# Attention of the chosen tokens: the products with V in three pieces per four heads, the projection by Wo in four pieces, and stacks and turnings beside other heads

## The chip, the cores and the metric

The kernel is one program on one core of a Trainium2 chip. The metric is the device time of one execution in microseconds (us). It is compared as the median of several runs of each kernel.

## The reference, cut to what matters

The program computes `x + attention(layernorm(x)) + sparse_layer(layernorm(x))` for 8192 rows of 512 numbers. The sparse layer picks the 1023 rows with the largest router weight and gives them a full transformer layer. The change lies in the attention of that layer:

```python
def heads(t):
    return t.reshape(b, kc, H, hd).transpose(0, 2, 1, 3)
q = rope(heads(hn @ wq), pos_sel)          # kc = 1023, H = 16, hd = 32
kk = rope(heads(hn @ wk), pos_sel)
v = heads(hn @ wv)
sc = jnp.einsum('bhqd,bhkd->bhqk', q, kk) / np.sqrt(hd)
sc = sc + m_sel[:, None]
a = jax.nn.softmax(sc, axis=-1)
o = jnp.einsum('bhqk,bhkd->bhqd', a, v).transpose(0, 2, 1, 3).reshape(b, kc, d) @ wo
x1 = x_sel + o
x2 = x1 + jax.nn.gelu(rmsnorm(x1, ln2) @ w1) @ w2
```

## The kernel before

The program has three phases, one after the other: the linear attention of all rows, the preparation of the chosen rows (their K, Q, V), and the attention and MLP of the chosen rows. The stage that the change touches is the attention, in a trace from about 1404 to 1745 us.

The 1023 chosen rows are 8 tiles of 128 queries, t = 0 to 7. Each tile goes through 16 heads, h = 0 to 15, against all 1023 keys. Each engine has its own instruction list, written out in this order; nothing is rescheduled, an engine that meets an unfulfilled wait stands. One turn of the loop `for h in range(H)` is called step h below. In step h:

- TensorE (PE) computes the scores of head h+2 into one of two PSUM pairs `Sp` (`score`, L2141; it waits until VectorE has read head h's scores out of the same pair), then perhaps some products with V (`values`, L2167), then turns head h-1's weights in two halves into `Tp[0]` (L2149) and `Tp[1]` (L2153), each half after its copy of the head before has been taken, then perhaps something extra.
- VectorE (DVE) adds the mask to the scores of head h, writes them to `Sm` and finds the least of each row ("the reduce", L2088, 1023 wide), then copies the second half of the turned head h-2 out of `Tp[1]` (`take_t`, L2038), then perhaps something extra.
- ScalarE (ACT) takes the exponential of head h in `Sm` (L1986), then copies the first half of the turned head h-1 (L1959), then perhaps something extra.

The products with V of four heads (a group g; 32 matmuls of 128 rows by 32 columns in fp32, k = 0 to 7 blocks of keys) go into the one PSUM tile `Op`. Before, they are issued in two pieces of 16, k = 0 to 3 and k = 4 to 7, in steps 4g+5 and 4g+6.

All the rest of a tile shares one PSUM tile `Wp`: the four attention groups turned back (`back`, L2177), the rows weighted by 1/sum (`attention_rows` on DVE, L2053) and turned `again` (L2183), the projection by Wo (`project`, L2190, four fp32 matmuls of 512 columns), the residual sum and the second norm on DVE (`second_norm`: step 0 the sum, L2060; step 1 the squares and a first guess of the root; steps 2 and 3 three Newton rounds, 9 tiny instructions, L1362 to L1364; step 4 the scaling, L2071), the normed rows turned (`norm_t`, L2198) for the MLP, and the four query stacks of the next tile (`stack`, L2211; their input `qst` is written by ACT, L1967, and DVE, L2044). The `PTs` buffer holds turned weights of five heads. In the last tile DVE also prepares the finished rows (`keep`, L2075 and L2076).

## Time and profile before

| what | value |
|---|---|
| time, median of 3 runs | 1948.97 us (1943.88 to 1950.05) |
| profiled execution: its time | 1945.36 us |
| profiled execution: its span | 1943.6 us |
| TensorE busy in the span | 95% |
| DVE / ACT busy in the span | 74% / 45% |
| granted TensorE clock, mean | 0.985 |
| attention stage | about 1404 to 1745 us |

The profiled execution is 3.6 us under the median of the runs. Busy shares are means over stages with different limits. In the attention stage every engine follows the same head loop, so its time is read from the starts of instructions: the distance from one start to the next on an engine is what an instruction costs there, also where the printed durations of neighbours overlap.

### The profile page before, as it was taken

What the parts mean: (1) busy time and instruction counts of PE and PEld (TensorE: products, weight loads), DVE (VectorE), ACT (ScalarE), POOL (GpSimd) and SP (SyncE); (2) the same over time, 40 slices, a digit from 0 to 9 for tenths busy, and PEclk for the clock granted to TensorE, in tenths of its full rate; (3) what the DMA queues carried; (4) which work ended last, traced back from release to release, by engine and by line L of the source; (5) the groups of instructions that cost most, each with busy time, mean ns of one, the idle gap of its engine ahead of it and who ended that gap; (6) DMA issues with size and microseconds to landing.
All of it is one profiled execution on the core that took longest, in us unless ns stands there. A gap on an engine that the chain in (4) does not pass through costs nothing. (4 is left out here: it accounts for less than half of the span.)

```text
span 1943.6 us, 72290 instructions
## 1 busy us (share of the span) xinstructions
PE 1848.5 (95%) x32348; PEld 1567.1 (81%) x32348; DVE 1445.2 (74%) x3477; ACT 875.7 (45%) x1494; POOL 148.7 (8%) x179
## 2 busy tenths in 40 slices
PE   6999999999999999999999999879899999879998
PEld 5888888888888888888888888657677777667997
DVE  6888788888887777787777777667588788876222
ACT  4443334343434443444434343325588787764110
POOL 2000000000000000000000000041100000001000
PEclk9999999999999999999999999879999999999999
DMA  4111211121121112111111110236500000015000
GB/s 147 47 46 58 73 52 46 58 74 52 46 74 52 36 36 61 43 36 40 59 41 36 47 51 30 95 95 183 164 26 12 13 12 23 13 41 161 17 12 22
DMA packets 65139, 108.45 MB, mean 56 GB/s; under 512 B 4720, under 2 KB 25216, under 8 KB 64832
## 3 DMA queue, kind: packets, MB, share of 16 engines
q1 hardware_dynamic: 59056, 84.69, 14.0%
q0 software_dynamic: 5776, 19.15, 3.2%
q8 instruction: 256, 4.19, 0.9%
q14 instruction: 51, 0.42, 0.1%
HBM read 59.26 MB, written 27.26 MB: 45 GB/s over the span
## 5 line engine op out<-in xcount | busy, mean ns | idle before, releaser
L1083 PE MATMUL proj<-xnT_high,held 128*128 128x256 f32 x1536 | 235.2, 288 | 3.3 <-DVE xnT_low L782 2.4
L1083 PEld LDWEIGHTS proj<-xnT_high,held 128*128 128x128 f32 x1536 | 203.6, 191 | 9.2 <-DVE xnT_low L782 2.9
L444 POOL TENSOR_TENSOR xs<-xs 128x512 f32<-128x512 f32 x63 | 80.9, 1285 | 1170.0 <-DVE xs L885 1170.0
L1083 PE MATMUL proj<-xnT_low,held 128*128 128x256 f32 x1024 | 163.7, 281 | 0.0
L2088 DVE CUSTOM_DVE_ANT_0 Sm<-Sp,held 128x1023 f32<-128x1023 f32 x128 | 155.5, 1216 | 8.0 <-DVE xs L2076 2.0
L1986 ACT ACTIVATE Sm<-Sm,least 128x1023 f32<-128x1023 f32 x128 | 146.7, 1146 | 14.1 <-DVE least L2088 13.3
L1083 PEld LDWEIGHTS proj<-xnT_low,held 128*128 128x128 f32 x1024 | 140.1, 190 | 0.0
L2141 PE MATMUL Sp<-KS,held 128*128 128x512 f32 x256 | 94.4, 451 | 29.9 <-DVE least L2088 25.6
L506 ACT ACTIVATE Pq<-Pq 128x1024 f32<-128x1024 f32 x63 | 66.9, 1062 | 123.4 <-DVE Pq L848 123.3
L486 ACT ACTIVATE QT<-proj 128x512 f32<-128x512 f32 x64 | 38.1, 595 | 182.4 <-PE proj L1083 182.4
L2038 DVE COPY PTs<-Tp 128x512 f32<-128x512 f32 x128 | 88.3, 690 | 29.7 <-PE Tp L2153 29.2
L465 ACT ACTIVATE DV<-proj 128x512 f32<-128x512 f32 x64 | 38.2, 598 | 160.1 <-PE proj L1093 160.1
L2362 PEld LDWEIGHTS Sp<-held,KS 128*128 128x128 f32 x768 | 95.3, 190 | 6.1 <-issue 3.6
L1959 ACT ACTIVATE PTs<-Tp 128x512 f32<-128x512 f32 x128 | 76.2, 595 | 52.4 <-PE Tp L2149 49.2
L2362 PE MATMUL Sp<-held,KS 128*128 128x256 f32 x768 | 96.8, 282 | 2.6 <-PEq L1863 2.0
L2422 PE MATMUL yb<-w2m,held 128*128 128x512 f32 x384 | 94.5, 396 | 0.0
L486 ACT ACTIVATE KT<-proj 128x512 f32<-128x512 f32 x64 | 38.2, 598 | 99.8 <-PE proj L1083 99.8
L2422 PEld LDWEIGHTS yb<-w2m,held 128*128 128x128 f32 x384 | 70.2, 189 | 14.9
L2149 PE MATMUL Tp<-ident,Sm 128*128 128x128 f32 x512 | 81.0, 281 | 1.0 <-ACT PTs L1959 0.9
L1083 PE MATMUL proj<-xnT_high,wk_low 128*128 128x256 f32 x512 | 81.2, 280 | 0.0
L2153 PE MATMUL Tp<-ident,Sm 128*128 128x128 f32 x512 | 77.4, 274 | 1.6 <-DVE PTs L2038 1.6
L848 DVE TENSOR_TENSOR Pq<-S,mx 128x1024 f32<-128x1024 f32 x63 | 77.2, 1225 | 2.1
(343 smaller groups left out, 4341.2 us busy)
## 6 DMA issues: line engine op xcount, KB each, us to landing
VS<-DV SPq DMA_DIRECT2D x64, 264.0 KB, 3.9
xs<-in_x SPq DMA_DIRECT2D x32, 512.0 KB, 4.8
out_rows<-xs SPq DMA_DIRECT2D x64, 256.0 KB, 2.0
mask_columns<-x1T SPq DMA_DIRECT2D x16, 512.0 KB, 5.2
xs<-in_w SPq DMA_DIRECT2D x16, 512.0 KB, 3.8
xe<-in_x SPq DMA_DIRECT2D x15, 512.0 KB, 3.5
QT<-in_wqT SPq DMA_DIRECT2D x1, 1024.0 KB, 6.5
KT<-in_wkT SPq DMA_DIRECT2D x1, 1024.0 KB, 9.4
```

Source lines behind the costliest of these rows:

```text
L444: pool.tensor_tensor(Ass[k], T1s[k], T2s[k], ALU.add).then_inc(s_as, 1)
L486: act.activation(raw[:, pn, 2 * k:2 * k + 2, :], v, ACT.Copy, scale=scale)
L848: dve.tensor_tensor(Pqs[k].rearrange("p g j k -> p j g k"), s_half(a), mx[:, :, :].rearrange("p j (g o) -> p j g o", o=1).broadcast_to([P, ...
L1083: ins = pe.matmul(bank[:, g * BT:g * BT + BT], w[hw][:, c, o:o + P], xnT[hx][:, c, :], start=n + c == 0, stop=n == 2 and c == G - 1)
L1986: act.activation(Sm[:, h % 4, 0:KC], Sm[:, h % 4, 0:KC], ACT.Exp, bias=least[:, h % 4:h % 4 + 1], scale=-1.0, accum_out=rsum[:, b, h:h + 1 ...
L2038: dve.tensor_copy(PTs[:, slot(t, h), 4:8, :], Tp[1][:, :].rearrange("p (k q) -> p k q", k=4))\
L2088: dve.tensor_tensor_reduce(Sm[:, h % 4, 0:KC], Sp[h % 2][:, 0:KC], mc[:, b, 0:KC], 1.0, 3.0e38, ALU.add, ALU.min, least[:, h % 4:h % 4 + 1])\
L2141: ins = pe.matmul(Sp[h % 2][:, u * 512:u * 512 + 512], QS[:, h, :], KS[:, h, u * 512:u * 512 + 512], start=True, stop=True)
L2149: ins = pe.transpose(Tp[0][:, k * P:k * P + P], Sm[:, h % 4, k * P:k * P + P], ident[:, :])
L2153: ins = pe.transpose(Tp[1][:, (k - 4) * P:(k - 4) * P + P], Sm[:, h % 4, k * P:k * P + P], ident[:, :])
L2362: ins = pe.matmul(self.hb[n % 4][:, e * self.NT:e * self.NT + self.NT], self.w1[hw][:, c, f * P:f * P + P], self.xT[hx][:, c, :], start=m ...
L2422: ins = pe.matmul(yb[(u % 2) * QU + q][:, :], gT[hg][:, n % 4, e, q * P:q * P + P], w2[hw][:, f, :], start=f + m == 0, stop=f == FC - 1 an ...
```

## The change

What it does, for a tile t (steps are those of tile t unless another is named):

- The products with V of a group go in three pieces, of 12, 12 and 8 matmuls, in steps 4g+5, 4g+6 and 4g+7. The first piece waits for ACT's copies alone, the second for DVE's too. ACT's `take_o` follows one step later. `PTs` is split into two tensors, one for each writer, with 5 and 6 slots.
- The projection goes in four pieces of one matmul, in steps 9 to 12, in place of one piece in step 8. `back` moves from step 3 to 6 and `again` from 6 to 7.
- The stacks of the next tile, all in steps 10 to 13 before, go to step 4 (first), 14 and 15 (second and third) and to step 0 of the next tile (fourth). ACT writes `qst` in step 1 in place of step 0; DVE's part stays in step 2.
- `norm_t` moves from step 15 to step 2 of the next tile but one loop turn (`norm_t(t - 2)` in tile t).
- On DVE, `attention_rows` moves from step 5 to step 7 and ahead of that step's copy; `second_norm` steps 0, 1, 2 move from steps 9, 10, 13 to 13, 14, 15, and its steps 3 and 4 from steps 13 and 14 to step 0 of the tile after.

```diff
-SLOTS = 5
-PTs = sb("PTs", [P, SLOTS, Q, P], c=c2_)
+QH = Q // 2
+SLOTS = (5, 6)
+PIECES = ((0, 1, 2), (3, 4, 5), (6, 7))
+PARTS = len(PIECES)
+PTs = [sb(f"PTs{e}", [P, SLOTS[e], QH, P], c=c2_) for e in range(2)]
...
-            if h == 2 and before:
+            if h == 3 and before:
                 take_o(t - 1, G - 1)
-            if h in (6, 10, 14):
+            if h in (7, 11, 15):
                 take_o(t, h // 4 - 1)
             if h > 0:
                 take_t(t, h - 1)
             elif before:
                 take_t(t - 1, H - 1)
-            if h == 1 and before and t >= 2:
+            if h == 0 and before:
+                take_stack(t, G - 1)
+            if h == 1 and after:
+                stack(t + 1)
+            if h == 2 and before and t >= 2:
                 take_x1(t - 2)
-            if h == 7 and before:
+            if h == 4 and after:
+                take_stack(t + 1, 0)
+            if h == 8 and before:
                 take_on(t - 1)
-            if h == 0 and after:
-                stack(t + 1)
-            if 10 <= h < 14 and after:
-                take_stack(t + 1, h - 10)
+            if h == 14 and after:
+                take_stack(t + 1, 1)
+            if h == 15 and after:
+                take_stack(t + 1, 2)
...
+            if h == 7 and before:
+                attention_rows(t - 1)
             if h > 1:
                 take_t(t, h - 2)
             elif before:
                 take_t(t - 1, H - 2 + h)
                 if h == 1:
                     weights(t - 1, 1 - b)
+            if h == 0 and t >= 2:
+                second_norm(t - 2, 3)
+                second_norm(t - 2, 4)
             if h == 2 and after:
                 stack(t + 1)
-            if h == 5 and before:
-                attention_rows(t - 1)
-            if h == 9 and before:
+            if h == 13 and before:
                 second_norm(t - 1, 0)
-            if h == 10 and before:
+            if h == 14 and before:
                 second_norm(t - 1, 1)
-            if h == 13 and before:
+            if h == 15 and before:
                 second_norm(t - 1, 2)
-                second_norm(t - 1, 3)
-            if h == 14 and before:
-                second_norm(t - 1, 4)
-            if not after and (h < Q - 2 or h == 13):
+                if not after:
+                    second_norm(t - 1, 3)
+                    second_norm(t - 1, 4)
+            if not after and (h < Q - 2 or h == 14):
                 keep(min(h, Q - 2))
...
         if part == 0:
+            pe.wait_ge(s_oc, t * G + (g + 1))
             pe.wait_ge(s_ta, t * H + (4 * g + 5))
+        if part == 1:
             pe.wait_ge(s_td, t * H + (4 * g + 5))
-            pe.wait_ge(s_oc, t * G + (g + 1))
-        for k in range(part * (Q // 2), (part + 1) * (Q // 2)):
+        for k in PIECES[part]:
+            e = k // QH
             n = P if k < Q - 1 else P - 1
             for j in range(4):
                 h = 4 * g + j
                 ins = pe.matmul(Op[DK * j:DK * j + DK, 0:P], V[0:n, k, h * DK:h * DK + DK],
-                                PTs[0:n, slot(t, h), k, :], start=k == 0, stop=k == Q - 1)
-        if part == 1:
-            ins.then_inc(s_pv, 1)
+                                PTs[e][0:n, slot(t, h, e), k % QH, :], start=k == 0, stop=k == Q - 1)
+        ins.then_inc(s_pv, 1)
 
     def back(t):
         pe.wait_ge(s_oc, t * G + (G + 1))
-        if t:
+        if t < Q - 2:
+            pe.wait_ge(s_qs, (t + 2) * G + 1)
+        else:
             pe.wait_ge(s_x1, t)
...
-    def project(t):
-        pe.wait_ge(s_w, 16)
-        pe.wait_ge(s_otc, t + 1)
-        for g in range(G):
+    def project(t, gs):
+        if gs[0] == 0:
+            pe.wait_ge(s_w, 16)
+            pe.wait_ge(s_otc, t + 1)
+        for g in gs:
             ins = pe.matmul(Wp[:, :], OnT[:, g, :], wo[:, g, :], start=g == 0, stop=g == G - 1)
-        ins.then_inc(s_wo, 1)
+        if gs[-1] == G - 1:
+            ins.then_inc(s_wo, 1)
...
-    def stack(t, g, first=False):
-
+    def stack(t, g):
 
         if g == 0:
             pe.wait_ge(s_ql, t + 1)
-            if not first:
-                pe.wait_ge(s_xc, t - 1)
+        if g == 0 and t > 2:
+            pe.wait_ge(s_x1, t - 2)
+        elif g == 1 and t > 1:
+            pe.wait_ge(s_xc, t - 1)
         else:
             pe.wait_ge(s_qs, t * G + g)
         for j in range(4):
...
-            if h % 4 in (1, 2) and h > 2:
-                values(t, (h - 5) // 4, h % 4 - 1)
-            elif h in (1, 2) and before:
+            if h % 4 and h > 3:
+                values(t, h // 4 - 1, h % 4 - 1)
+            elif h % 4 and before:
                 values(t - 1, G - 1, h - 1)
             if h > 0:
                 turn_p(t, h - 1)
             elif before:
                 turn_p(t - 1, H - 1)
-            if before and h == 3:
+            if h == 0 and before:
+                stack(t, G - 1)
+            if h == 2 and t >= 2:
+                norm_t(t - 2, True)
+            if h == 4 and after:
+                stack(t + 1, 0)
+            if h == 6 and before:
                 back(t - 1)
-            if before and h == 6:
+            if h == 7 and before:
                 again(t - 1)
-            if before and h == 8:
-                project(t - 1)
-            if after and 10 <= h < 14:
-                stack(t + 1, h - 10, first=not before)
-            if before and h == 15:
-                norm_t(t - 1, after)
+            if 9 <= h < 13 and before:
+                project(t - 1, (h - 9,))
+            if h >= 14 and after:
+                stack(t + 1, h - 13)
...
     turn_p(Q - 1, H - 1)
-    values(Q - 1, G - 1, 0)
-    values(Q - 1, G - 1, 1)
+    norm_t(Q - 2)
+    for part in range(PARTS):
+        values(Q - 1, G - 1, part)
```

On PE the order around the projection shows the first two points. Before, from step 7 on in a middle tile (`Sp` scores, `Op` products with V, `Tp` turned heads, `Wp<-wo` projection):

```order
L2141 MATMUL Sp<-KS,held 128x512 x2
L2149 MATMUL Tp<-ident,Sm 128x128 x4
L2153 MATMUL Tp<-ident,Sm 128x128 x4
L2141 MATMUL Sp<-KS,held 128x512 x2
L2149 MATMUL Tp<-ident,Sm 128x128 x4
L2153 MATMUL Tp<-ident,Sm 128x128 x4
L2190 MATMUL Wp<-wo,OnT 128x512 x4
L2141 MATMUL Sp<-KS,held 128x512 x2
L2167 MATMUL Op<-PTs,V 32x128 x16
L2149 MATMUL Tp<-ident,Sm 128x128 x4
L2153 MATMUL Tp<-ident,Sm 128x128 x4
```

The changed kernel on PE, the last rows of step 9 to step 12 of the same tile:

```order
L2206 MATMUL Wp<-wo,OnT 128x512
L2153 MATMUL Sp<-KS,held 128x512 x2
L2181 MATMUL Op<-PTs,V 32x128 x12
L2161 MATMUL Tp<-ident,Sm 128x128 x4
L2165 MATMUL Tp<-ident,Sm 128x128 x4
L2206 MATMUL Wp<-wo,OnT 128x512
L2153 MATMUL Sp<-KS,held 128x512 x2
L2181 MATMUL Op<-PTs,V 32x128 x8
L2161 MATMUL Tp<-ident,Sm 128x128 x4
L2165 MATMUL Tp<-ident,Sm 128x128 x4
L2206 MATMUL Wp<-wo,OnT 128x512
L2153 MATMUL Sp<-KS,held 128x512 x2
```

The projection no longer stands as one block; one matmul of it follows the turned head of each of four steps, and three of these steps also hold a piece of the products with V.

On DVE the order around the end of a tile shows the norm. Before, the end of step 13 and step 14 (`ISA Sm` is the reduce, `COPY PTs` the copy, `t<-r`, `t<-t,v`, `r<-t,r` one Newton round; the last of three rounds is shown, and the scaling of step 14 behind it):

```order
L1362 SCALAR_TENSOR_TENSOR t<-r 128x1
L1363 TENSOR_TENSOR t<-t,v 128x1
L1364 SCALAR_TENSOR_TENSOR r<-t,r 128x1
L2088 ISA Sm,least<-Sp,held 128x1023
L2088 ISA least 128x1
L2038 COPY PTs<-Tp 128x512
L2071 SCALAR_TENSOR_TENSOR On<-xs,r,ln 128x512
L2088 ISA Sm,least<-Sp,held 128x1023
```

The changed kernel on DVE, the last Newton round of step 15, step 0 of the next tile and step 1 up to the reduce of step 2:

```order
L1364 SCALAR_TENSOR_TENSOR r<-t,r 128x1
L2097 ISA Sm,least<-Sp,held 128x1023
L2097 ISA least 128x1
L2047 COPY PTs<-Tp 128x512
L1362 SCALAR_TENSOR_TENSOR t<-r 128x1
L1363 TENSOR_TENSOR t<-t,v 128x1
L1364 SCALAR_TENSOR_TENSOR r<-t,r 128x1
L2080 SCALAR_TENSOR_TENSOR On<-xs,r,ln 128x512
L2097 ISA Sm,least<-Sp,held 128x1023
L2097 ISA least 128x1
L2047 COPY PTs<-Tp 128x512
L2058 RECIPROCAL rinv<-rsum 128x16
```

The third Newton round and the scaling now stand in step 0, directly ahead of the steps that hold the reciprocal and DVE's part of the next query stack.

On ACT the write of `qst` (`held<-xs`) moves behind one more exponential and copy. In the changed kernel, steps 1 and 2:

```order
L1989 ACTIVATE Sm,rsum<-Sm,least 128x1023
L1962 ACTIVATE PTs<-Tp 128x512
L1970 ACTIVATE held<-xs 128x16x64
L1989 ACTIVATE Sm,rsum<-Sm,least 128x1023
L1962 ACTIVATE PTs<-Tp 128x512
L1983 ACTIVATE x1T<-Wp 128x4x128
```

Before, the same write stood behind the copy of step 0. It now stands one step ahead of the DVE instruction that reads its result.

## Rows read from the trace of the kernel before

**Rows 1.** The page, its first line: the span.

```profile
span 1943.6 us, 72290 instructions
```

**Rows 2.** Windows, one tile: busy us (instructions) by engine, then PEclk, DMA share, GB/s.

```profile
1549.53:1590.93 41.40, 39.17 (x454) 29.89 (x453) 34.53 (x66) 32.63 (x59) 0.95 (x1) 1.00 0.05 14
```

**Rows 3.** Waits of 1400 to 1745 us: total us, times, longest.

```profile
DVE PTs L2038 <- PE Tp L2153: 29.2, 42, 1.2
PE Sp L2141 <- DVE least L2088: 25.6, 53, 1.8
...
DVE xs L2060 <- PE Wp L2190: 19.2, 7, 2.7
```

**Rows 4.** Timeline of PE: start, us, line, operands [idle before, releaser]; steps 1 to 6.

```profile
1571.89 0.60 PE L2153 MATMUL Tp<-ident,Sm 128*128 128x128 f32 x4
...
1575.64 0.70 PE L2141 MATMUL Sp<-KS,held 128*128 128x512 f32 x2 [0.65 <-DVE least L2088]
1576.18 0.60 PE L2149 MATMUL Tp<-ident,Sm 128*128 128x128 f32 x4
1576.62 0.60 PE L2153 MATMUL Tp<-ident,Sm 128*128 128x128 f32 x4
1577.06 0.60 PE L2177 MATMUL Wp<-ident,OTs 128*128 128x128 f32 x4
1577.41 0.71 PE L2141 MATMUL Sp<-KS,held 128*128 128x512 f32 x2
...
1579.23 0.71 PE L2141 MATMUL Sp<-KS,held 128*128 128x512 f32 x2 [0.23 <-DVE least L2088]
1579.87 1.08 PE L2167 MATMUL Op<-PTs,V 128*32 128x128 f32 x32
1580.88 0.66 PE L2149 MATMUL Tp<-ident,Sm 128*128 128x128 f32 x4
...
1581.73 0.71 PE L2141 MATMUL Sp<-KS,held 128*128 128x512 f32 x2
```

**Rows 5.** Timeline of DVE, steps 2 and 3 of the same tile.

```profile
1572.53 0.69 DVE L2038 COPY PTs<-Tp 128x512 f32<-128x512 f32 x1 [0.64 <-PE Tp L2153]
1573.13 1.22 DVE L2044 TENSOR_TENSOR held<-xs,held 128x1024 fp32r<-128x1024 f32 x1
1574.27 1.22 DVE L2088 CUSTOM_DVE_ANT_0 Sm<-Sp,held 128x1023 f32<-128x1023 f32 x1
...
1575.41 0.69 DVE L2038 COPY PTs<-Tp 128x512 f32<-128x512 f32 x1
```

**Rows 6.** Timeline of PE, the projection (step 8) in two tiles.

```profile
1546.50 3.60 PE L2190 MATMUL Wp<-wo,OnT 128*128 128x512 f32 x8
1549.53 1.02 PE L2141 MATMUL Sp<-KS,held 128*128 128x512 f32 x2
...
1587.90 3.60 PE L2190 MATMUL Wp<-wo,OnT 128*128 128x512 f32 x8
```

**Rows 7.** Timeline of DVE, the norm in steps 9 to 14.

```profile
1550.13 0.69 DVE L2060 TENSOR_TENSOR xs<-Wp,xs 128x512 f32<-128x512 f32 x1 [2.74 <-PE Wp L2190]
...
1553.23 0.68 DVE L2063 CUSTOM_DVE_ANT_0 On<-xs 128x512 f32<-128x512 f32 x1
...
1554.52 1.22 DVE L2088 CUSTOM_DVE_ANT_0 Sm<-Sp,held 128x1023 f32<-128x1023 f32 x1 [0.21 <-DVE r L1360]
...
1559.91 0.15 DVE L1362 SCALAR_TENSOR_TENSOR t<-r 128x1 f32<-128x1 f32 x1
...
1561.83 1.22 DVE L2088 CUSTOM_DVE_ANT_0 Sm<-Sp,held 128x1023 f32<-128x1023 f32 x1 [0.21 <-DVE r L1364]
...
1563.58 0.74 DVE L2071 SCALAR_TENSOR_TENSOR On<-xs,r,ln 128x512 f32<-128x512 f32 x1
```

**Rows 8.** Timeline of ACT, steps 0 and 1: copy and `qst`.

```profile
1569.15 0.60 ACT L1959 ACTIVATE PTs<-Tp 128x512 f32<-128x512 f32 x1
1569.65 1.05 ACT L1967 ACTIVATE held<-xs 128x1024 fp32r<-128x1024 f32 x1
```

**Rows 9.** Timeline of DVE, end of tile 7: last reduce, last copy.

```profile
1738.34 1.22 DVE L2088 CUSTOM_DVE_ANT_0 Sm<-Sp,held 128x1023 f32<-128x1023 f32 x1
...
1742.57 0.69 DVE L2038 COPY PTs<-Tp 128x512 f32<-128x512 f32 x1 [0.96 <-PE Tp L2153]
```

More of the change, by code:

```diff
@@ L1909, in feed_forward, with slot, read_before @@
             KC = K - 1
-            def slot(t, h):
-                return (t * H + h) % SLOTS
-            def read_before(eng, t, h):
-                n = t * H + h - SLOTS
+            def slot(t, h, e):
+                return (t * H + h) % SLOTS[e]
+            def read_before(eng, t, h, e):
+                n = t * H + h - SLOTS[e]
                 if n >= 0:
-                    eng.wait_ge(s_pv, n // 4 + 1)
+                    eng.wait_ge(s_pv, n // 4 * PARTS + 2 + e)
             def tile(t):
@@ L1957, in take_t @@
                     act.wait_ge(s_t, t * (2 * H) + (2 * h + 1))
-                    read_before(act, t, h)
-                    act.activation(PTs[:, slot(t, h), 0:4, :], Tp[0][:, :].rearrange("p (k q) -> p k q", k=4),
+                    read_before(act, t, h, 0)
+                    act.activation(PTs[0][:, slot(t, h, 0), :, :], Tp[0][:, :].rearrange("p (k q) -> p k q", k=4),
                                    ACT.Copy).then_inc(s_ta, 1)
                 def take_o(t, g):
-                    act.wait_ge(s_pv, t * G + (g + 1))
+                    act.wait_ge(s_pv, PARTS * (t * G + g + 1))
                     act.activation(OTs[:, g, :], Op[:, 0:P], ACT.Copy).then_inc(s_oc, 1)
@@ L2036, in take_t @@
                     dve.wait_ge(s_t, t * (2 * H) + (2 * h + 2))
-                    read_before(dve, t, h)
-                    dve.tensor_copy(PTs[:, slot(t, h), 4:8, :], Tp[1][:, :].rearrange("p (k q) -> p k q", k=4))\
+                    read_before(dve, t, h, 1)
+                    dve.tensor_copy(PTs[1][:, slot(t, h, 1), :, :], Tp[1][:, :].rearrange("p (k q) -> p k q", k=4))\
                        .then_inc(s_td, 1)
@@ L2254, in _ @@
                 again(Q - 1)
-                project(Q - 1)
+                project(Q - 1, range(G))
                 up.hidden(pe, 2)
```

## The prediction

> **What bounds the kernel now.** First the page for the size of things: a span of 1943.6 us [rows 1], of which the stage that is changed has about 340 (the table above). Then the windows: one tile lasts 41.40 us, which is also the distance between two projections, 1546.50 to 1587.90 [rows 6], at full granted clock (1.00, the 2.4 GHz level), with PE busy 39.17, DVE 34.53, ACT 32.63 us [rows 2]. PE looks full, but then the waits: 53 times its scores waited for the reduce on DVE, 25.6 us in all, while DVE waited 42 times for turned heads (29.2 us) and seven times 2.7 us for the projection [rows 3]. So the stage is a pair of engines that take turns, and a busy share says too little. The timeline gives the rules of the turns.
>
> PE, start to start: a score takes 0.55 (1575.64 to 1576.18), the first half of a turned head 0.44, the second 0.36 when a score follows, so a light step is 1.35. Something of four transposes behind it adds 0.44 (1576.62 to 1577.06 to 1577.41). A step with 16 products with V takes 2.50 (1579.23 to 1581.73), 1.15 more: 1.01 for the products (1579.87 to 1580.88) and 0.14 for the joint. [rows 4] The projection takes 3.03 plus 0.31, since the score behind it lasts 1.02 in place of 0.71, so 3.34 [rows 6].
>
> DVE: the reduce of step h starts at R. The score of step h on PE starts at R + 1.37 or later (1574.27 to 1575.64) [rows 4, 5]. The copy starts at R + 1.15 or 0.64 after the second half of the turned head of PE's step before starts (1571.89 to 1572.53), whichever is later, and costs 0.60 [rows 4, 5]. So DVE needs 1.78 per step without extras, more than PE's light step of 1.35; and DVE can't run ahead, since `Sp` has two buffers.
>
> A tile of before walked by these rules, step 9 to step 9 of the next tile, comes out as the trace has it: starts of the scores within 0.05 us, and 41.4 in all. PE's own work in that is 16 x 1.35 + 8 x 1.15 + 7 x 0.44 + 3.4 = 37.3; the other 4.1 are stalls in steps 2, 4, 7, 10, 13, 15 and 0. This is the tool for the forecast.
>
> **The change, part by part.** All for one middle tile.
>
> Products with V: 12, 12 and 8 matmuls cost 0.76, 0.76 and 0.51 by the 1.01 for 16, and a joint of 0.14 each: steps of 2.25, 2.25 and 2.00. Four more joints: +0.56 on PE. Projection: four pieces of 0.84 and a boundary of 0.08 each (0.44 in place of 0.36 in front): 0.92 each, +0.3. PE's work becomes 16 x 1.35 + 8 x 0.90 + 4 x 0.65 + 7 x 0.44 + 4 x 0.92 = 38.2. The bound from below for joints is nothing.
>
> A rule of the Trainium skill speaks against these joints (TensorE: Matmul & The Clock Gate, Architectural detail: the array is 16x 32x32): the queue pulls weight loads ahead of matmuls in flight. By it the split would be free and PE's work would stay at 37.3. The row shows 0.14 at each border of differing groups, so I take that.
>
> DVE, extras in order, each start to start: residual sum 0.61, squares and first guess 1.29 (1553.23 to 1554.52), nine Newton instructions 1.92 of which 0.19 is the last wait, so three cost 0.58 and six with the wait 1.34; scaling 0.66, by its 0.74 less the overlap of 0.08 that the copy shows [rows 7]; its part of the query stack 1.14 [rows 5]. Their sum hardly changes. Their places do: the residual sum to step 13, then 1.29 in 14, 1.34 in 15, 0.58 + 0.66 = 1.24 in step 0, the reciprocal (an unmoved cost, 0.46 in the walk) in step 1, 1.14 in step 2. Before, the norm stood in steps 9, 10, 13 and 14, three of which hold products with V.
>
> ACT: `qst` now follows the copy of step 1. In the walk PE's first half of step 1 starts 1.40 after the score, the copy about 0.7 after that, 0.50 later `qst` starts and takes 1.05 [rows 8]; DVE, ready for its part 3.1 after the score of step 1, gets it at 3.65. That is a new wait of 0.5 us per tile, and the reduce of step 3 stands behind it on DVE. Before, `qst` was done a whole step earlier.
>
> **The walk.** Starts of the scores, step 9 at 0. Steps 9 to 12 are PE's: 3.17, 6.34, 9.26, 11.52 for steps 10 to 13. The long waits for the projection on DVE and ACT go, as intended, since it no longer stands in a block. The sum on DVE starts at 11.8, the reduce of step 14 at 12.4, the score at 13.79. From here DVE sets the pace, and its reduces start at 15.94, 19.06, 22.08, 24.32 and, behind the new wait, 28.24 for steps 15, 0, 1, 2, 3. The scores follow at 17.31, 20.43, 23.45, 25.70, 29.61, with stalls on PE of 0.8, 0.7, 1.2 and, in step 2, 1.2. Step 3 and 4: 29.61, 31.61; step 5 at 33.86 after a stall of 0.46 (a light step behind one with products, as now); 36.11; 38.80; in step 7 PE turns its head only after DVE has weighted the rows and then copied (0.4), step 8 at 41.65, again light (0.4), step 9 at 43.43.
>
> So a tile takes 43.4 in place of 41.4: 38.2 of work and 5.3 of stalls against 37.3 and 4.1. **+2.0 us a tile.** Behind the evening out of PE stands an uneven DVE: between the reduces of steps 14 and 3 it needs 15.8 us, PE has 11.9 us of work there; between 3 and 13 it is the other way round.
>
> Ends: tile 0 has no norm and no projection. The walk gives the wait for `qst` (+0.45) and then a gain from the pieces, 0.8 by its end, and step 3 of tile 1 starts 0.5 earlier than before. Five tiles from there to step 3 of tile 6: 5 x 2.03 = +10.1, so +9.6. In tile 7 step 0 holds the scaling and last round beside `keep`: +1.3; `attention_rows` leaves step 5: -0.6; steps 6 to 9 with neither block: -1.9; the remainder of the way to that tile's first reduce +0.5. At step 9: +8.9. At its end the last reduce comes 10.3 later; the norm of tile 6 now stands whole behind it (2.4 us of round and scaling), so the last copy starts 5.6 after that reduce where it was 4.2 (1738.34 to 1742.57) [rows 9]: +1.4. The MLP then starts as before, its first products wait for that chain. Sum: 10.3 + 1.4 = **+11.7 us**. The profiled execution took 1945.36, 3.6 less than the median; against the median of 1948.97 this gives 1960.7.
>
> **Rivals.** (A) As walked: 1960.7; own range 1955 to 1966, by joints free (-1.6 in the stage) or steps of the ACT chain adding half a microsecond a tile more. (B) Joints free and ACT's copy earlier, so no wait for `qst`: 7 x 0.5 + 1.6 less, +6.6, 1955.6; with each of three stalls a little smaller, +4, 1953. For it: the 0.14 is read at one kind of border. Against it: a score, a transpose and a product all show such a border. (C) It evens out: the 2.7 us a tile that DVE waited for the projection, and the stall of PE in the steps behind it, go and come back in the same size elsewhere: 1949. (D) Faster: only PE counts. Then a tile is 38.2 of work and 1.3 of stalls in steps 4, 7 and 8, 39.5, so -1.9 for each of six tiles: 1938. It is decided in steps 14 to 2: DVE would have to be 4 us shorter there, or its reduce be let ahead. For it: 29.2 us of DVE's waits [rows 3] do lie in steps with products. Against it: these waits are spare time of an engine that now gets its extras where none is spare. (E) ACT late as well: its exponentials of steps 0 and 2 slide behind `take_stack` and `qst` until PE waits for them, +1 a tile more: 1968. In the walk they keep 1 us and more of slack.
>
> **The numbers.** Chances: A 0.69, B 0.13, C 0.05, D 0.08, E 0.05. A change of 0.3%, 5.8 us, is about what a measurement of this kernel can tell from none. B falls half under it, so faster 0.08, same 0.12, slower 0.80. The range 1950 to 1968 holds A, B and most of E and leaves out D and half of C.
>
> **What would show it.** Right: a tile of 43 to 43.8 us between two projections; PE waits for the reduce in steps 14 to 2 of 0.5 to 1 us, shown shorter by 0.24 than the stall (0.23 shown for 0.47 here [rows 4]); DVE without idle time there except before its query stack part; no 2.7 us wait before the residual sum. Wrong: a tile under 41.4, so the reduce must be able to start before the extras' time has passed; or DVE idle in steps 15 to 2. If the wait before DVE's part of the stack is absent, the price falls by 3.5 us.

## The result, and the profile after

| kernel | median of runs, us | ratio to before | 95% interval |
|---|---|---|---|
| before | 1949.51 (1943.88 to 1958.05) | | |
| after | 1962.14 (1960.49 to 1966.93) | 1.0062 | 1.0046 to 1.0078 |

The change costs 12.1 us; +11.7 and 1960.7 were predicted. The profiled execution took 1961.97 us, close to its median, at a mean granted clock of 0.983 (before 0.985). First the page of after, its first line and the first line of its busy times (engine, busy us, share, instructions):

```profile
span 1960.2 us, 72291 instructions
PE 1858.5 (95%) x32348; PEld 1564.8 (80%) x32348; DVE 1445.5 (74%) x3477; ACT 878.5 (45%) x1494; POOL 148.8 (8%) x179
```

The shares are those of before; they tell nothing. One tile does. The windows of after: the same tile as in [rows 2], then two parts of it, from step 15 to the start of step 3 and from there to step 9 (length; busy us of PE, PE's weight loads, DVE, ACT, POOL; granted clock, DMA share, GB/s):

```profile
1551.54:1595.10 43.56, 40.19 (x453) 29.29 (x453) 34.63 (x67) 33.16 (x61) 0.94 (x1) 1.00 0.05 14
1569.00:1582.00 13.00, 10.62 (x126) 7.79 (x129) 11.24 (x26) 10.59 (x18) 0.85 (x1) 1.00 0.15 42
1582.00:1595.00 13.00, 12.69 (x150) 9.67 (x142) 10.38 (x19) 10.56 (x21) 0.00 (x0) 1.00 0.01 2
```

The tile takes 43.56 us in place of 41.40 at the full granted clock (1.00, the 2.4 GHz level); DVE's busy time is the same to 0.1 us, PE's is 1.0 more, and PE's idle time is 3.37 where it was 2.23. What came to the idle time lies in the first part: there PE is idle for 2.38 of 13.00 us, in the other for 0.31. The same two parts of the tile of before:

```profile
1565.71:1575.64 9.93, 8.99 (x111) 6.75 (x110) 8.77 (x15) 9.06 (x17) 0.95 (x1) 1.00 0.17 54
1575.64:1590.93 15.29, 14.82 (x140) 11.05 (x141) 11.91 (x20) 12.17 (x22) 0.00 (x0) 1.00 0.01 2
```

The waits of after, 1400 to 1765 us (total, times, longest):

```profile
DVE PTs L2047 <- PE Tp L2165: 50.1, 64, 1.5
...
PE Sp L2153 <- DVE least L2097: 28.9, 41, 2.6
...
DVE On L2062 <- PE Wp L2192: 9.2, 8, 2.5
...
DVE held L2053 <- ACT held L1970: 3.4, 6, 0.6
...
DVE xs L2069 <- PE Wp L2206: 1.2, 7, 0.2
```

Beside [rows 3]: the wait for the projection has gone, as intended (19.2 us, now 1.2). But the wait for turned heads has grown from 29.2 to 50.1, and two new ones stand beside it, for the groups turned back (`On`) and for ACT's part of the query stack (`held`). The four rows of DVE add up to 63.9; 2.5 of this (the longest wait for `On`) lies behind the stage, where before has the same wait outside the window of its rows, so 61.4 compares with the 48.4 of the two rows of before. DVE has the same work in a longer stage, so it waits more, only for something else. PE's own wait has grown from 25.6 to 28.9 in fewer, longer pieces (41 for 53), printed 0.24 shorter each than the stall.

The timeline of PE in after, step 9, and then the scores at the start of steps 15, 0, 1, 2 and 3 of the same turn (start, us, line, operands, count [idle before, releaser]):

```profile
1551.54 0.71 PE L2153 MATMUL Sp<-KS,held 128*128 128x512 f32 x2 [0.16 <-DVE least L2097]
1552.18 0.86 PE L2181 MATMUL Op<-PTs,V 128*32 128x128 f32 x24
1552.98 0.66 PE L2161 MATMUL Tp<-ident,Sm 128*128 128x128 f32 x4
1553.47 0.60 PE L2165 MATMUL Tp<-ident,Sm 128*128 128x128 f32 x4
1553.90 1.02 PE L2206 MATMUL Wp<-wo,OnT 128*128 128x512 f32 x2
1554.37 1.03 PE L2153 MATMUL Sp<-KS,held 128*128 128x512 f32 x2
...
1568.79 0.71 PE L2153 MATMUL Sp<-KS,held 128*128 128x512 f32 x2 [0.58 <-DVE least L2097]
...
1571.87 0.71 PE L2153 MATMUL Sp<-KS,held 128*128 128x512 f32 x2 [0.33 <-DVE least L2097]
...
1574.86 0.70 PE L2153 MATMUL Sp<-KS,held 128*128 128x512 f32 x2 [0.97 <-DVE least L2097]
...
1577.14 0.71 PE L2153 MATMUL Sp<-KS,held 128*128 128x512 f32 x2
...
1581.18 0.70 PE L2153 MATMUL Sp<-KS,held 128*128 128x512 f32 x2 [1.08 <-DVE least L2097]
```

And DVE in steps 0 to 3:

```profile
1570.49 1.22 DVE L2097 CUSTOM_DVE_ANT_0 Sm<-Sp,held 128x1023 f32<-128x1023 f32 x1 [0.21 <-DVE r L1364]
...
1571.64 0.69 DVE L2047 COPY PTs<-Tp 128x512 f32<-128x512 f32 x1
1572.25 0.15 DVE L1362 SCALAR_TENSOR_TENSOR t<-r 128x1 f32<-128x1 f32 x1
...
1572.82 0.76 DVE L2080 SCALAR_TENSOR_TENSOR On<-xs,r,ln 128x512 f32<-128x512 f32 x1
1573.49 1.22 DVE L2097 CUSTOM_DVE_ANT_0 Sm<-Sp,held 128x1023 f32<-128x1023 f32 x1
...
1577.42 0.69 DVE L2047 COPY PTs<-Tp 128x512 f32<-128x512 f32 x1 [0.50 <-PE Tp L2165]
1578.67 1.23 DVE L2053 TENSOR_TENSOR held<-xs,held 128x1024 fp32r<-128x1024 f32 x1 [0.56 <-ACT held L1970]
1579.81 1.21 DVE L2097 CUSTOM_DVE_ANT_0 Sm<-Sp,held 128x1023 f32<-128x1023 f32 x1
```

From 1570.49 to 1573.49 DVE goes without a pause from the reduce of step 0 through its copy, three Newton instructions and the scaling to the reduce of step 1, and the score on PE stands 1.37 behind each reduce (1573.49 to 1574.86). Then, behind a wait of 0.50 for a turned head that wasn't foretold (1577.42), the predicted new wait: 0.56 before DVE's part of the query stack, on ACT's part; the reduce of step 3 comes behind it, and PE's wait of 1.08 behind that.

Starts of the scores, step 9 at 0, as predicted and as they came:

| step | 11 | 13 | 14 | 15 | 0 | 1 | 2 | 3 | 5 | 7 | 9 |
|---|---|---|---|---|---|---|---|---|---|---|---|
| predicted | 6.34 | 11.52 | 13.79 | 17.31 | 20.43 | 23.45 | 25.70 | 29.61 | 33.86 | 38.80 | 43.43 |
| after | 5.97 | 11.10 | 13.70 | 17.25 | 20.33 | 23.32 | 25.60 | 29.64 | 33.96 | 38.96 | 43.56 |
| before | 6.37 | 9.96 | 13.68 | 16.18 | 18.44 | 20.18 | 22.72 | 26.11 | 29.70 | 35.14 | 41.40 |

After and before are level at step 14. The loss of a tile arises from there to step 3 (+3.5, in 15.9 us), and 1.4 of it comes back from step 3 to step 9.

Below, "the stage" is the time from the first score to the first MLP product, read from each kernel's trace, and "a tile" is the distance of step 9 of two middle tiles. The median less the stage is 1607.6 us before (1608.1 with the later median) and 1607.2 after, and 1604.3 to 1609.8 over all kernels here, so the stage explains the medians to within about 3 us. (1948.97 is the first median of before, from 3 runs; 1949.51 the one with the runs that came later.)

Stage and tile are read from one execution of each kernel. The tile is the steadier of the two: the middle tiles of after differ by 0.02 us, and experiment 6 repeats them (43.55). The medians are coarser. Of the experiments built on after, only the ratios of 3, 5 and 9 have intervals apart from that of after (1.0046 to 1.0078); those of 1, 2, 6, 7 and 11 overlap it. What a single edit is worth is therefore shown by the tile, and by the stage with the reserve above, not by the median.

### The profile page after: what moved, and what is told of

The parts are those of the page before. It is cut to its first block and busy times, and to the rows that moved or that the text cites. A ratio compares the mean times of both kernels' runs of the same rounds, so it can differ in the third digit from the quotient of the medians.

```text
span 1960.2 us, 72291 instructions
## 1 busy us (share of the span) xinstructions
PE 1858.5 (95%) x32348; PEld 1564.8 (80%) x32348; DVE 1445.5 (74%) x3477; ACT 878.5 (45%) x1494; POOL 148.8 (8%) x179
## 5 line engine op out<-in xcount | busy, mean ns | idle before, releaser
L2153 PE MATMUL Sp<-KS,held 128*128 128x512 f32 x256 | 101.8, 481 | 33.9 <-DVE least L2097 28.9
L2047 DVE COPY PTs<-Tp 128x512 f32<-128x512 f32 x128 | 88.1, 689 | 50.3 <-PE Tp L2165 50.1
L2153 PEld LDWEIGHTS Sp<-KS,held 128*128 128x128 f32 x256 | 41.8, 194 | 60.4 <-issue 50.6
L486 ACT ACTIVATE KT<-proj 128x512 f32<-128x512 f32 x64 | 38.2, 598 | 100.2 <-PE proj L1083 100.2
```

The lines of the kernel that those rows point to most:

```text
L486: act.activation(raw[:, pn, 2 * k:2 * k + 2, :], v, ACT.Copy, scale=scale)
L2047: dve.tensor_copy(PTs[1][:, slot(t, h, 1), :, :], Tp[1][:, :].rearrange("p (k q) -> p k q", k=4))\
L2153: ins = pe.matmul(Sp[h % 2][:, u * 512:u * 512 + 512], QS[:, h, :], KS[:, h, u * 512:u * 512 + 512], start=True, stop=True)
```

## The experiments

**1. The stack's input a step earlier.** ACT writes its part `qst` in step 0 in place of 1. Nothing else.

```diff
-                        if h == 1 and after:
+                        if h == 0 and after:
                             stack(t + 1)
```

> The changed kernel, with ACT's write of the next tile's query stack back in step 0 (behind the fourth stack's copy). Theory (uneven DVE plus a new wait for this write): the idle time of DVE before its part of the stack (3.4 us in 6 waits in the changed kernel) goes, and with it 0.5 us in each of 7 tiles: -3.5 us, a tile of 43.0 us. Rival (the wait is not on the path, PE's more numerous groups are the price): no change, a tile stays at 43.55.

Measured: 1957.3 us, ratio 1.0042 (1.0025 to 1.0059), stage -3.3 (351.72), a tile 42.90 (-0.65). No wait of DVE on `qst` is left. The wait was real and cost about what the prediction said (0.5 a tile, 3.5 in the stage).

**2. The norm where DVE waits.** The three Newton rounds and the scaling of tile t-2 move to steps 10 and 11 of tile t; its turning `norm_t` and ACT's copy move to step 13. In the last tile the rounds and scaling of tile 5 stand in step 0, those of tile 6 in step 15 as in after. Waits keep `h2` of one tile from being overwritten.

```diff
-                        if h == 0 and t >= 2:
+                        if h == (10 if after else 0) and t >= 2:
+                            second_norm(t - 2, 2)
+                        if h == (11 if after else 0) and t >= 2:
                             second_norm(t - 2, 3)
...
                         if h == 15 and before:
-                            second_norm(t - 1, 2)
                             if not after:
+                                second_norm(t - 1, 2)
```

> The changed kernel, with the Newton rounds and the scaling of a tile's norm moved out of steps 15 and 0 into steps 10 and 11 of the next tile, where DVE stands idle, and the turning of the normed rows from step 2 to step 13 (tile 7 apart). No instruction is added or left out, one wait is. Theory (uneven DVE): the walk gives a tile of 41.5 us in place of 43.5, for five tiles: -9.5 us. Rival (PE's joints are the price): -1 us at most, since PE's list holds the same groups. Rival (the steps 10 and 11 have no room): slower.

Measured: 1958.73 us, ratio 1.0053 (1.0036 to 1.007), stage -6.05 (348.94), a tile 41.98 (-1.57). Right in direction, but 9.5 was expected: the tile gave 1.57 of 2.0, the stage 6.05, and the medians of after and of this kernel differ by 3.4 only (by the ratios 1.8), so that the gain in the program's time isn't shown by itself. Five tiles of 1.57 are 7.9; the interval from tile 6 to 7 gave 1.8 back (51.06 in place of 49.22), where the last tile holds more of the norms of two tiles. And the wait for `qst` doesn't shrink when DVE comes sooner, DVE waits for ACT as before. The timeline of DVE in this kernel, steps 2 and 3:

```profile
1571.93 0.69 DVE L2047 COPY PTs<-Tp 128x512 f32<-128x512 f32 x1 [0.64 <-PE Tp L2168]
1573.18 1.23 DVE L2053 TENSOR_TENSOR held<-xs,held 128x1024 fp32r<-128x1024 f32 x1 [0.56 <-ACT held L1970]
1574.33 1.22 DVE L2098 CUSTOM_DVE_ANT_0 Sm<-Sp,held 128x1023 f32<-128x1023 f32 x1
```

**3. Both edits together.**

> The changed kernel with both edits of the two runs before. Theory: the two prices add, a tile of 41.0 us, -13 us against the changed kernel, about 1949 and so level with the kernel before. Rival (the waits hide behind one another): no more than the larger of the two alone.

Measured: 1951.33 us, ratio 1.0011 (1.0000 to 1.0022), stage -10.45 (344.54), a tile 41.33 (-2.22). A tile is as short as before the change; with the late `qst` gone and the norm where DVE waits, three quarters of the stage's loss of 13.6 are gone. The two gains add up to the hundredth (0.65 + 1.57 = 2.22). This isn't yet what moving the norm had cost, for the place that it has here is better than the one before the change, as the next run shows.

**4. The same idea in the kernel before.** There DVE waited 2.7 us for the projection in each tile. Now it does three parts of the norm of tile t-2 in that time, and nothing of it in steps 13 and 14.

```diff
+                        if h == 9 and 2 <= t < Q - 1:
+                            for step in (2, 3, 4):
+                                second_norm(t - 2, step)
...
-                        if h == 13 and before:
+                        if h == 13 and t >= Q - 2:
                             second_norm(t - 1, 2)
```

> The kernel before, in which only the norm is moved: its Newton rounds and scaling from steps 13 and 14 to step 9 of the next tile, ahead of the residual sum, where DVE waits 2.7 us for the projection as one block; the turning of the normed rows follows in step 9. Theory (what counts is where DVE's extras stand): a tile of 40.6 in place of 41.4 us in five tiles, -4 us against the kernel before. Rival (PE is the bound and DVE's extras are covered): no change. Rival (the longer chain in step 9 delays the residual sum and the stacks): slower by 1 to 3 us.

Measured: 1945.51 us, ratio 0.9988 (0.9975 to 1.0001), stage -1.1 against before (340.32), a tile 40.85 (-0.55); the interval of the ratio holds 1. The tile is near what was expected, the stage isn't. From step 3 of tile 1 to step 3 of tile 6 it gains 2.6 us; 0.3 are lost in the stage's first steps, where the code is that of before, 0.2 between step 3 of tile 6 and step 9 of tile 7, and 0.95 behind that, where the last tiles hold more of the norm. The timeline of DVE shows the idle time filled; before, the same sum had 2.74 in front [rows 7]:

```profile
1546.42 0.75 DVE L2072 SCALAR_TENSOR_TENSOR On<-xs,r,ln 128x512 f32<-128x512 f32 x1
1547.51 0.69 DVE L2060 TENSOR_TENSOR xs<-Wp,xs 128x512 f32<-128x512 f32 x1 [0.34 <-PE Wp L2196]
```

**5 and 6. The same load in two places.** Six tiny dependent instructions on DVE whose result nobody uses, once in step 15, where DVE is said to set the pace, and once in step 10, where it waits. The kernel is after; the two differ by one number.

```diff
+                        if h == 15 and before:
+                            for _ in range(6):
+                                link(dve.tensor_tensor(spare[:, :], spare[:, :], spare[:, :], ALU.mult))
```

> The changed kernel with six tiny DVE instructions added in step 15 of tiles 1 to 7, each waiting for the one before (about 0.19 us each, 1.2 in all, the size of two Newton rounds); their result is used by nothing. Theory (DVE sets the pace from step 14 to 3): +1.2 us in each of 7 tiles, +8 us against the changed kernel, a tile of 44.7. Rival (PE sets it everywhere): no change.

> The same six instructions in step 10 of tiles 1 to 7, where DVE is idle for 1.3 us per tile in the changed kernel. Theory: no change against the changed kernel (within 1 us). Rival (any DVE work counts): +8 us as in step 15.

Measured, step 15: 1971.03 us, ratio 1.0113 (1.0095 to 1.0131), stage +9.4 (364.42), a tile 44.69 (+1.13). Step 10: 1961.55 us, ratio 1.0070 (1.0054 to 1.0086), stage +0.2 (355.19), a tile 43.55 (the same). Where the load of step 10 went, the waits tell: DVE waits 40.6 us for turned heads here, 50.1 in after. The timeline of DVE, step 10:

```profile
1552.65 0.69 DVE L2048 COPY PTs<-Tp 128x512 f32<-128x512 f32 x1 [0.86 <-PE Tp L2170]
1553.26 1.12 DVE L2116 TENSOR_TENSOR spare<-spare 128x1 f32<-128x1 f32 x6
1554.59 1.22 DVE L2098 CUSTOM_DVE_ANT_0 Sm<-Sp,held 128x1023 f32<-128x1023 f32 x1 [0.21 <-DVE spare L2116]
```

This separates the two accounts most sharply. If PE alone counted (rival D), neither would cost anything; if DVE's sum counted, both would. The two kernels ran together, and their medians are 9.5 us apart. (Of the +9.4 in the stage 7.0 have come by step 9 of tile 7, about six tiles of 1.13; the 2.4 behind it are 1.3 more than the one load that is left, which wasn't traced further.)

**7. Products with V in two pieces again, in after** (`back` then in step 5).

```diff
-            PIECES = ((0, 1, 2), (3, 4, 5), (6, 7))
+            PIECES = ((0, 1, 2, 3), (4, 5, 6, 7))
...
-                        if h % 4 and h > 3:
+                        if h % 4 in (1, 2) and h > 3:
```

> The changed kernel with the products with V again in two pieces of 16 (steps 4g+5 and 4g+6), the turning back in step 5; projection, stacks, norm and buffers as in the changed kernel. Theory: the pieces hardly matter, since half of them lie in steps in which DVE sets the pace: -0.4 us a tile, -3 us against the changed kernel. Rival (the four more joints a tile are the price): their 0.56 us a tile and the stalls behind them go, and most of the loss with them. Rival (the pieces are a gain): slower.

Measured: 1959.77 us, ratio 1.0057 (1.0042 to 1.0073), stage -3.5 (351.51), a tile 42.80 (-0.75). The gain lies between step 3 and step 9 (-0.9; the other part loses 0.1), and perhaps not all of it is the pieces'. The run also moves `back` from step 6 to 5, and with this goes a wait that DVE has in step 7 of after, in seven tiles together 6.8 us:

```profile
1590.78 0.69 DVE L2062 TENSOR_TENSOR On<-Wp,rinv 128x512 f32<-128x512 f32 x1 [0.89 <-PE Wp L2192]
```

The copy and the reduce of step 8 stand behind it (1591.99), and the score 1.37 behind that (1593.36), so step 7 takes 2.86 where PE has 2.44 of work (2.00 + 0.44). Walked by the prediction's rules without this wait, step 7 ends 0.4 earlier, and of that 0.3 is left at step 9, where the copy of step 8 waits for its turned head instead. So up to 0.3 of the 0.75 may be the place of `back`, an estimate; no run moves it alone.

**8. Products with V in three pieces, in before** (`PTs` split, `back` in step 4, `take_o` a step later, all else as before).

> The kernel before with the products with V in three pieces alone (two PTs tensors, ACT's copies of the groups one step later, the turning back in step 4). Theory, by the walk: a tile of 42.1 in place of 41.4 us, +5 us against the kernel before: steps of 2.25 and 2.00 where DVE already sets the pace, and the joints on PE. Rival (evening out the products removes DVE's waits): -3 us or more. Rival (neither): no change.

Measured: 1954.46 us, ratio 1.0041 (1.0026 to 1.0057), stage +8.5 against before (349.92), a tile 42.56 (+1.16; two of the middle intervals are 42.8). Expected were 0.7 a tile and 5 us; what came is more than the joints. A step that was light and now holds a third piece takes 2.50 in place of 1.77 (step 11) or 2.06 in place of 1.77 (step 3), and the two others, made 4 products lighter each, don't give that back: by step 5 the tile is 1.2 late (30.89 for 29.70, step 9 at 0).

**9. After, with all three undone or mended**: the stack's input in step 0, the norm in steps 10 and 11 (tiles 6 and 7 keep their own parts), V in two pieces. Of the change this leaves the projection in four pieces, the separate `PTs` buffers and the new places of the stacks, of `again` and of `attention_rows`.

> The changed kernel with the query stack's write in step 0 of ACT, the rounds and the scaling of the norm in steps 10 and 11 of the next tile (tiles 6 and 7 apart, which stay as in the changed kernel) and the products with V in two pieces. Left of the change: the projection in four pieces and the places of the stacks and turnings. Theory: the gains of the single runs add up, a tile of 40.6 us and the stage from the first score to the first MLP product at 339 us, against 355.0 in the changed kernel and 341.4 before: -2 us against the kernel before. Rival (once DVE is relieved PE waits elsewhere): between 341 and 345 us, no gain over before.

Measured: 1945.66 us, ratio 0.9981 (0.9971 to 0.9990), stage 338.32, a tile 40.61. Of its waits, 1400 to 1765 us, the one of PE for the reduce is a third shorter than in after (28.9):

```profile
PE Sp L2157 <- DVE least L2098: 18.8, 38, 2.6
```

**10. Before, as in 4, with DVE's part of the query stack in step 7**, ahead of that step's copy, out of step 2.

```diff
+                        if h == 7 and after:
+                            stack(t + 1)
...
-                        if h == 2 and after:
-                            stack(t + 1)
```

> The kernel before with the norm in the idle step 9, as in the run before of that name, and also DVE's part of the next query stack moved from step 2 to step 7 ahead of its copy, where DVE waits 0.7 us for a turned head. Theory: the stall of 0.9 us behind step 2 goes, 0.5 comes back behind step 7: a tile of 40.5 in place of 40.9, stage 338.5 us, -3 us against the kernel before. Rival (the idle time before a copy can't be used, since the reduce behind it is late all the same): stage of 340.3 or longer.

Measured: 1946.0 us, ratio 0.9980 (0.9971 to 0.9990), stage 337.82, a tile 40.77. As fast as experiment 9; both are faster than before by 0.2%, a small gain, with intervals that leave out 1.

**11. The projection in one piece again, in after** (step 9).

```diff
-                        if 9 <= h < 13 and before:
-                            project(t - 1, (h - 9,))
+                        if h == 9 and before:
+                            project(t - 1, range(G))
```

> The changed kernel with the projection again in one block, in step 9 behind the turned head; the residual sum stays in step 13. Theory (walk): a block of 3.3 us in one step makes steps 11 to 13 wait for DVE, +0.8 us a tile, +5 us against the changed kernel: the split of the projection is the part of the change that gains. Rival (the boundaries of the pieces are the price of the change): -0.3 us a tile, -2 us.

Measured: 1966.22 us, ratio 1.0087 (1.0072 to 1.0103), stage +6.9 (361.92), a tile 44.45 (+0.89). In this kernel cutting the projection helps. The waits of this kernel show why: a block of 3 us on PE makes both others wait, up to 4 us at a time (1.5 and 1.4 in after).

```profile
ACT PTs L1962 <- PE Tp L2161: 69.4, 82, 4.0
DVE PTs L2047 <- PE Tp L2165: 59.5, 58, 3.9
```

Of the 6.9, 4.5 are five tiles of 0.89, 1.5 come between step 3 of tile 6 and step 9 of tile 7 (tile 6 to tile 7 takes 50.74 where it took 49.22), and 0.9 behind that.

**The parts of a tile**, each measured in after: the late `qst` 0.65 (experiment 1), the norm where it stands against the steps in which DVE waits 1.57 (2), V in three pieces with the later `back` 0.75 (7), projection in four -0.89 (11). And experiment 9, which mends the first three, is 2.95 shorter than after where they make 2.97. So these three hardly act on each other in after. In before the third piece of V costs 1.16 and not 0.75, so this holds near after alone.

The sum is +2.08, close to the +2.15 of the change, but it doesn't explain it to that degree. The norm is measured against a place that before doesn't have either: there the same move gains 0.55 (experiment 4). And after with all four taken out would by the sums have a tile of 43.55 - 2.97 + 0.89 = 41.47, an estimate, where before with its norm in the idle step has 40.85. So about 0.6 a tile belongs to the rest of the change (the places of the stacks, turnings and `attention_rows`, the split of `PTs`), which no run takes out by itself. The 0.6 and the 0.55 stand on opposite sides; that they cancel is chance.

## Why the prediction was right

**The whole.** 11.7 us predicted, 12.1 by the ratio, 13.6 in the stage of the profiled executions. Case A came, close to its middle.

**PE's work 38.2 in place of 37.3.** Measured is a busy time of 1.02 more (39.17 to 40.19), and the steps fit: steps 10 and 11 take 3.14 and 2.93, walked 3.17 and 2.92. Step 9 takes 2.83 (1551.54 to 1554.37) and was walked as 3.17, step 13 takes 2.60 and was walked as 2.27: the longer score stands behind a piece of the projection, in the next step, so the 0.92 of each piece is shifted and the sum holds (13.70 and 13.79 at step 14). The pieces: twelve products (24 records) take 0.80 from start to start (1552.18 to 1552.98) where 0.76 was taken from 1.01 for 16, so a piece is 0.04 dearer than its share, and eight pieces of twelve 0.3 a tile. The rule of the Trainium skill that was weighed (TensorE: Matmul & The Clock Gate, Architectural detail: the array is 16x 32x32) says that weight loads can be pulled ahead of matmuls in flight. That the split would then be free is what the prediction drew from it, and that didn't come: experiment 7 gets 0.75 a tile by taking four borders away (`back` moved with them), experiment 8 loses 1.16 by adding them. Whether weight loads were pulled ahead at these borders no run here shows. The row was the better guide. Its 0.56 of PE's work and, in rival B, 1.6 us in the stage for free joints were too low: experiment 7 gives 3.5.

**Stalls 5.3 in place of 4.1.** The places came out: PE waits 0.58, 0.33, 0.97 and 1.08 (shown 0.24 short, so stalls of 0.8, 0.6, 1.2 and 1.3) ahead of the scores of steps 15, 0, 1 and 3; the walk had 0.8, 0.7, 1.2 and 1.2. It took 1.78 for a plain step of DVE where its own 1.15 and 0.60 make 1.75, which is 0.1 over these steps. The uneven DVE as their cause is shown by experiments 5 and 6: six instructions of 1.12 us cost 1.13 a tile where DVE sets the pace, and nothing where it waits. This is also what refutes rival D.

**The wait for `qst`, 0.5 a tile, 3.5 in the stage.** 0.56 in the row, -0.65 a tile and -3.3 in experiment 1. With the 12.1 us of the whole this rules out rival B, by which this wait was absent. The whole rules out C too: what DVE waited for the projection did come back elsewhere, but more of it than went. Rival E, a late ACT, didn't come either: over the stage of after PE's matmuls wait for ACT's copies once, 0.8 us, and never for an exponential; before they waited for the copies three times, 1.7 us.

**Tile +2.0.** It is +2.15 (43.55). From step 3 of tile 1 to step 3 of tile 6 the prediction had +10.1, and +10.9 came.

**Ends.** From the first score to step 3 of tile 1 the prediction had -0.5; it is +0.38. This is the step that was most off, by 0.9. It says that `qst` is waited for in tile 0 (+0.45) and that the pieces then gain 0.8 by that tile's end. At step 14 of tile 0 after is in fact 0.74 ahead of before. It loses 0.5 of this by step 2 of tile 1 and the other 0.64 in step 3, and there stands a second wait for `qst`, in tile 1, which the forecast's account of this end doesn't name (whether the walk behind it had it can't be told from what it shows):

```profile
1448.02 1.23 DVE L2053 TENSOR_TENSOR held<-xs,held 128x1024 fp32r<-128x1024 f32 x1 [0.56 <-ACT held L1970]
```

Experiment 1, in which only `qst` is earlier, is 1.07 faster over this whole way: 0.44 by step 3 of tile 0 and 0.63 in step 3 of tile 1. So the wait was worth 1.07 in this term, where 0.45 was named. The rest of the 0.9, about 0.3, stays open.

TensorE's clock isn't the reason, though it looks like it. The windows from 4.5 to 10.5 us behind the first score, for after and then for experiment 2, whose code is that of after up to this point (columns as above):

```profile
1407.60:1413.60 6.00, 5.01 (x21) 4.27 (x20) 4.39 (x7) 4.12 (x8) 0.00 (x0) 0.63 0.33 123
```

```profile
1406.81:1412.81 6.00, 3.84 (x21) 3.17 (x20) 4.39 (x7) 4.11 (x8) 0.00 (x0) 0.85 0.34 128
```

The granted clock comes up from the 1.2 GHz level later in after (0.63 against 0.85), and both reach step 3 of tile 1 47.41 us behind their first score. Experiment 4 has the instructions of before up to this point, and its clock comes up later (0.55 in the third 3 us, 1.00 in before); there the way takes 47.37 in place of 47.03. So a late clock went with 0.3 in that kernel and with nothing in after.

The other end fits: between step 3 of tile 6 and step 9 of tile 7 -0.7 was predicted and -0.7 came, so that +8.9 there became +10.55 by the 0.9 and the 0.8 above; from there to the first MLP product +3.05 came, +2.8 was the forecast. The end of tile 7 in the timeline of DVE in after, beside [rows 9]:

```profile
1748.71 1.22 DVE L2097 CUSTOM_DVE_ANT_0 Sm<-Sp,held 128x1023 f32<-128x1023 f32 x1 [0.33 <-DVE xs L2085]
...
1752.20 0.75 DVE L2080 SCALAR_TENSOR_TENSOR On<-xs,r,ln 128x512 f32<-128x512 f32 x1
...
1754.76 0.69 DVE L2047 COPY PTs<-Tp 128x512 f32<-128x512 f32 x1 [1.21 <-PE Tp L2165]
```

The last copy comes 6.05 behind the last reduce where it was 4.23: the norm of tile 6 stands between them, as walked, but 0.4 longer than the 5.6 of the walk.

**Errors that cancelled.** The mechanism was right, and the stage was under-called by 1.9 (11.7 for 13.6): 0.9 at its start, 0.8 in the five tiles, 0.2 at its end. The 12.1 of the ratio is 1.5 less than the stage's 13.6: the medians differ by 12.6 only, and stage and median go together to within 3 us, as said above. That 11.7 lies 0.4 from 12.1, and 1960.7 within 1.4 of the median, is partly luck.

## What to carry to other kernels

When engines take turns in order with two buffers between them, neither busy shares nor sums of work tell the time: walk one period with starts from the trace, and look for the stretch in which one engine has more to do than the other. Small work of the engine that sets the pace in a stretch should go to a stretch in which it waits (here 1.13 us cost 1.13 or nothing, by its place alone). A block on the other engine for which the others wait up to 4 us was worth cutting (0.89 a tile); the products with V, pieces of 1.0 us, were not (0.75 and 1.16 lost, with all that moved along with them). Check each moved producer against the consumer of its data: one step too late here cost 0.65 us a tile.

## What was not expected of the hardware

The execution of after that was profiled is 16.6 us longer in its span than that of before. The stage has 13.6 of this, what lies ahead of it -1.4, and the rest, 4.4, is in the MLP, whose code the change doesn't touch. The timeline of ACT and of PE in after, in the same stretch:

```profile
1809.43 1.06 ACT L2366 ACTIVATE held<-x1T 128x1024 fp32r<-128x1024 f32 x1 [8.17 <-remote]
```

```profile
1811.80 4.43 PE L2385 MATMUL Sp<-held,KS 128*128 128x256 f32 x24 [2.78 <-DVE held L2370]
...
1818.87 2.96 PE L2385 MATMUL Sp<-held,KS 128*128 128x256 f32 x24
```

ACT is idle for 8.17 us until something that the trace calls remote; PE then is idle for 2.78, and its next 24 products take 4.43 where such a group takes 2.96, in all 4.2 us. In the first 2.0 us of these products the granted clock is 0.50, the 1.2 GHz level, after 1.00 ahead of the idle time:

```profile
1803.00:1809.00 6.00, 6.00 (x38) 5.05 (x36) 0.00 (x0) 0.00 (x0) 4.61 (x5) 1.00 0.73 208
1811.80:1813.80 2.00, 2.00 (x9) 2.00 (x10) 0.97 (x2) 0.00 (x0) 0.00 (x0) 0.50 0.00 0
```

Such a wait of ACT, of 7.9 to 9.6 us, stands in the profiles of all eleven experiments, those built on before too, and not in the one profile of before, where the same instruction has:

```profile
1794.05 1.06 ACT L2343 ACTIVATE held<-x1T 128x1024 fp32r<-128x1024 f32 x1 [5.00 <-PE Sp L2362]
```

So it isn't the change's. If it stands in most executions of before too, which one profile can't tell, it would also account for the 3.6 us by which the profiled execution of before was faster than its median. Eight gathers on POOL and one packet of instructions lie in the same stretch, but before has them too; what releases ACT stays open, and no run tried it.
